# A two-layer image network in fp32: the 3x3 convolution keeps its split planes in a ring, and its element work moves between VectorE, ScalarE and GpSimd

## What is computed

```python
x = x + _L0_conv_ref(_gn(x), ...)     # gate, windowed attention (8x8 windows, 16 heads), projection
x = x + _L1_conv_ref(_gn(x), W, bias) # 3x3 convolution, 128 -> 128 channels, padding 1, plus bias
```

## Time and profile before

| | |
|---|---|
| median of 3 runs | 1300.46 us (1294.46 to 1301.38) |
| profiled execution | 1303.66 us, its span 1301.9 us |
| busy: TensorE matmul | 1058.8 us (81%) |
| busy: VectorE | 1024.6 us (79%) |
| busy: ScalarE | 793.4 us (61%) |
| busy: GpSimd | 605.2 us (46%) |
| mean granted TensorE clock | 0.946 of full speed |

### The profile page before, as it was taken

One profiled execution on the slowest core, in us unless ns is written; L12 is line 12 of the kernel. 1 busy time (PEld: TensorE's weight loads), 2 busy tenths in 40 slices (PEclk: granted clock), 3 DMA queues, 4 the chain that ended last, 5 costly groups with the idle time before them and its releaser, 6 DMA issues. The chain is left out here.

```text
span 1301.9 us, 52825 instructions
## 1 busy us (share of the span) xinstructions
PE 1058.8 (81%) x23011; PEld 582.1 (45%) x23011; DVE 1024.6 (79%) x1315; ACT 793.4 (61%) x1295; POOL 605.2 (46%) x501
## 2 busy tenths in 40 slices
PE   1179999989998975887855999999999998498886
PEld 1045555555555542333322555555555555243332
DVE  6866787778887646999996677777787774599998
ACT  1147877777787764544412777777777776454442
POOL 7004444444444354555541344445445444366665
PEclk9999999999999996999885999999999999698998
DMA  7054444435444400222234544445444441001112
GB/s 284 25 147 122 134 130 132 140 113 145 123 133 127 138 19 1 97 98 97 97 114 139 138 130 137 127 128 140 133 132 129 138 141 30 1 33 48 49 50 80
DMA packets 114918, 140.60 MB, mean 108 GB/s; under 512 B 25088, under 2 KB 91008, under 8 KB 113664
## 3 DMA queue, kind: packets, MB, share of 16 engines
q1 hardware_dynamic: 114688, 137.23, 35.2%
HBM read 67.96 MB, written 67.11 MB: 104 GB/s over the span
## 5 line engine op out<-in xcount | busy, mean ns | idle before, releaser
L646 DVE TENSOR_REDUCE m_all<-ps 128x16 f32<-128x1024 f32 x256 | 312.8, 1222 | 134.2 <-PE ps L855 133.7
L369 POOL TENSOR_TENSOR g_lo<-work,g_hi 128x512 f16<-128x512 f32 x64 | 91.6, 1431 | 301.1 <-ACT g_hi L503 301.1
L361 POOL TENSOR_SCALAR work<-work 128x256 f32<-128x256 f32 x128 | 114.2, 892 | 210.2 <-DVE work L639 191.9
L824 PE MATMUL ps<-work,c_hi 128*128 128x512 f16 x384 | 153.5, 400 | 64.3 <-DVE work L744 64.3
L528 ACT CAST work<-work 128x640 f16<-128x640 f32 x128 | 91.9, 718 | 151.6 <-DVE work L740 118.0
L867 PE MATMUL ps<-q_bd,k_pl 128*64 128x256 f16 x2048 | 164.3, 283 | 18.2 <-DMA q_bd<-m_pair 13.0
L451 ACT ACTIVATE work<-ps,ws 128x1024 f32<-128x1024 f32 x128 | 142.7, 1115 | 40.8 <-PE ps L867 39.0
L855 PEld LDWEIGHTS ps<-k_pl,q_bd 48*64 48x64 f16 x8192 | 88.7, 111 | 155.1 <-issue 75.4
L744 DVE TENSOR_TENSOR work<-work 128x640 f16<-128x640 f32 x128 | 152.3, 1193 | 4.3 <-ACT work L528 4.2
L451 ACT ACTIVATE late_probs<-ps,ws 128x1024 f32<-128x1024 f32 x128 | 141.6, 1106 | 20.4 <-PE ps L867 20.4
L825 PE MATMUL ps<-work,c_lo 128*128 128x512 f16 x384 | 152.7, 398 | 0.0
(11 more groups left out here) (128 smaller groups left out, 2008.7 us busy)
## 6 DMA issues: line engine op xcount, KB each, us to landing
stack_scratch<-work SPq DMA_DIRECT2D x128, 256.0 KB, 2.0
k_pl<-stack_scratch SPq DMA_DIRECT2D x128, 192.0 KB, 3.7
q_bd<-stack_scratch SPq DMA_DIRECT2D x256, 96.0 KB
stack_scratch<-work SPq DMA_DIRECT2D x128, 128.0 KB, 2.1
out_dram<-work SPq DMA_DIRECT2D x32, 512.0 KB, 2.6
img<-in_x_dram SPq DMA_DIRECT2D x8, 1024.0 KB, 13.5
img<-in_x_dram SPq DMA_DIRECT2D x16, 512.0 KB, 4.2
q_bd<-m_pair SPq DMA_DIRECT2D x256, 8.0 KB
```

The lines of the kernel that those rows point to most:

```text
L361: g.tensor_scalar(near[h], near[h], -2.0, None, ALU.add).then_inc(less_done, 1)
L646: v.tensor_reduce(m_all[:, 0, :, p], ps[:, S_B:S_B + 2, :].rearrange("p r (a k) -> p (r a) k", k=WIN), AX.X, ALU.max).then_inc(max_done, 1)
L824: t_.matmul(o, lhs_hi, rhs_hi, start=first, stop=False)
```

## The change

- **Ring.** `x_hi` and `x_lo` become one tile `x_both` of 18 rows per plane. A strip needs 10 rows; even strips use rows 0 to 9, odd strips rows 8 to 17, so two rows serve both. `normed`, the planes, the casts and the remainders therefore handle 8 new rows (the first strip 9) instead of 10. After an odd strip the last two rows are copied to the front by `carry` on VectorE. An even strip's casts still wait for the strip before on TensorE, an odd strip's only for the carry.
- **All four planes** are made on VectorE (`plane_of`), none on GpSimd.
- **Sums.** ScalarE starts both output pixels from bank 1 (`bases`, two instructions; the odd pixel is kept with the opposite sign). VectorE adds banks 0 and 3 in one instruction of 2 x 512 elements (`ends`) and bank 2 to both pixels in another (`middle_sums`).
- **Residual** on GpSimd in two instructions of 512 elements, every second pixel each. Except in the last strips the first half also waits for plane 1 and the second for plane 3 of the strip three further on. The second subtracts, which turns the sign back.
- **Three output buffers**, and the statistics of a refilled strip are taken three strips later instead of two.
- `cx` lies on the first layer's `g_hi`/`g_lo` (`g_both`); `work` grows from 8468 to 9984 fp32 per partition. The zero row of the first strip is now in the fp16 ring.

The core of the diff. The lines that it takes away stand in the kernel above; here only what comes in their place:

```diff
-HALO = CROWS + 2
+XROWS = CROWS + 1
+RING = 2 * CROWS + 2
+OUTS = 3
...
+        g_both = sb("g_both", [P, BUFS * UT])
+        g_hi, g_lo = (g_both[:, :].bitcast(F16)[:, k * BUFS * UT:(k + 1) * BUFS * UT].rearrange("p (s t) -> p s t", s=BUFS)
+                      for k in range(2))
...
+        cx = g_both[:, 0:XROWS * WIDE].rearrange("p (r c) -> p r c", r=XROWS)
+        plane = [part(i * XROWS * (SIDE // 2), XROWS * (SIDE // 2)).rearrange("p (r c) -> p r c", r=XROWS) for i in range(PLANES)]
+        x_both = part(2304, PLANES * RING * (SIDE // 2)).bitcast(F16).rearrange("p (k i r c) -> p k i r c", k=2, i=PLANES, r=RING)
+        x_hi, x_lo = x_both[:, 0, :, :, :], x_both[:, 1, :, :, :]
+        c_out = [part(6912 + i * 1024, 1024).rearrange("p (r c) -> p r c", r=CROWS) for i in range(OUTS)]
...
+        def ring_rows(t):
+            at = CROWS * (t % 2)
+            return slice(at + (1 if t == 0 else 2), at + RING - CROWS)
+        def new_rows(t):
+            return slice(0 if t == 0 else 1, XROWS)
+        def column(t, s):
+            return cx[:, new_rows(t), s:s + SIDE - 1:2]
...
+        def halves(buf):
+            return buf.rearrange("p r (c e) -> p e (r c)", e=2)
...
+                    if more and t == CUNITS - 4:
+                        after(sp, cx_done, (b + 1) * CUNITS - 1)
+                        sp.wait_ge(kept_done, 2)
+                        for e in range(2):
+                            refill(CUNITS - 2 + e, x_in[e])
                     after(sp, cadd_done, n)
                     after(sp, out_done, n - 1)
+                    sp.dma_start(out[b, :, t * CROWS:t * CROWS + CROWS, :], c_out[n % OUTS][:, :, :]).then_inc(out_done, 16)
+                    if more and t < CUNITS - 2:
                         after(sp, cx_done, n + 1)
+                        after(sp, next_in, t - 1)
+                        refill(t, next_in)
...
+                def residual(t, n, spared):
+                    c = outputs_view(n)
+                    x1 = (kept[t - CUNITS + 2] if spared and t >= CUNITS - 2 else img[:, t * CROWS:t * CROWS + CROWS, :])
+                    x1 = x1.rearrange("p r (c e) -> p (r c) e", e=2)
+                    after(pool, sums_out, n)
+                    if t < CUNITS - 4:
+                        after(pool, planes_done, n + 3, 2)
+                    g.tensor_tensor(c[:, :, 0], c[:, :, 0], x1[:, :, 0], ALU.add).then_inc(cadd_done, 1)
+                    if t < CUNITS - 4:
+                        after(pool, planes_done, n + 3, 4)
+                    g.tensor_tensor(c[:, :, 1], x1[:, :, 1], c[:, :, 1], ALU.subtract).then_inc(cadd_done, 1)
...
+                def bases(n):
                     after(act, conv_done, n, 2)
+                    after(act, out_done, n - OUTS)
+                    for e, (col, bias) in enumerate(((R_CONV, vecs[:, 3:4]), (R_MINUS, cf[:, C_MINUS:C_MINUS + 1]))):
+                        a.activation(outputs(c_out[n % OUTS], e), ps[:, PLANES * (n % 2) + 1, :], ACT.Identity,
+                                     scale=ws[:, col:col + 1], bias=bias).then_inc(base_out, 1)
...
+                    def normed(t, n):
+                        after(act, planes_done, n - 1)
+                        last = XROWS - (1 if t == CUNITS - 1 else 0)
+                        r = slice(new_rows(t).start, last)
+                        a.activation(cx[:, r, 1:1 + SIDE], img[:, t * CROWS + r.start:t * CROWS + r.stop, :],
                                      ACT.Identity, scale=cf[:, C_SLOPE:C_SLOPE + 1], bias=cf[:, C_OFF:C_OFF + 1]).then_inc(cx_done, 1)
+                    def high(i, t, n):
+                        after(act, planes_done, n, i + 1)
+                        if t % 2 == 0:
+                            after(act, conv_done, n - 1, i + 1)
+                        elif t > 1:
+                            after(act, carried, carries(b, t - 2))
+                        a.copy(x_hi[:, i, ring_rows(t), :], plane[i][:, new_rows(t), :]).then_inc(x_hi_done, 1)
                     if top:
                         act.wait_ge(coef_ready, 2 * b + 2)
+                        normed(t, n)
+                        for i in range(PLANES):
+                            high(i, t, n)
+                        normed(t + 1, n + 1)
+                    if not top:
+                        bases(n - 1)
                     if not bottom:
+                        for i in range(PLANES):
+                            high(i, t + 1, n + 1)
+                    if t + 2 < CUNITS:
+                        normed(t + 2, n + 2)
+                    if bottom and b + 1 == BATCH:
+                        bases(n)
...
+                v.memset(x_both[:, :, :, 0, :].rearrange("p k i c -> p (k i) c"), 0.0).then_inc(pads_zero, 1)
...
+                def ends(n):
+                    bank = PLANES * (n % 2)
+                    after(dve, base_out, n)
+                    after(dve, conv_done, n)
+                    c = halves(c_out[n % OUTS])
+                    v.scalar_tensor_tensor(out=c, in0=ps[:, bank:bank + PLANES:PLANES - 1, :], scalar=ws[:, R_CONV:R_CONV + 1], in1=c,
+                                           op0=ALU.mult, op1=ALU.add).then_inc(ends_out, 1)
+                def middle_sums(n):
+                    after(dve, ends_out, n)
+                    c = halves(c_out[n % OUTS])
+                    v.scalar_tensor_tensor(out=c, in0=ps[:, PLANES * (n % 2) + 2, :].unsqueeze(1).broadcast_to([P, 2, 512]),
+                                           scalar=ws[:, R_CONV:R_CONV + 1], in1=c, op0=ALU.mult, op1=ALU.add).then_inc(sums_out, 1)
+                def sums(n):
+                    ends(n)
+                    middle_sums(n)
...
+                    def plane_of(i, t, n):
                         after(dve, cx_done, n)
+                        after(dve, x_lo_done, n - 1, i + 1)
+                        if t == CUNITS - 1 and i == 0:
+                            after(dve, planes_done, n - 1)
+                            v.memset(cx[:, XROWS - 1, 1:1 + SIDE], 0.0).then_inc(pads_zero, 1)
                             dve.wait_ge(pads_zero, 4 * b + 4)
+                        l, r, op = ((0, 2, ALU.subtract), (1, 2, ALU.add), (2, 1, ALU.subtract), (1, 3, ALU.subtract))[i]
+                        v.tensor_tensor(plane[i][:, new_rows(t), :], column(t, l), column(t, r), op).then_inc(planes_done, 1)
+                    def low(i, t, n):
                         after(dve, x_hi_done, n, i + 1)
+                        v.tensor_tensor(x_lo[:, i, ring_rows(t), :], plane[i][:, new_rows(t), :], x_hi[:, i, ring_rows(t), :],
+                                        ALU.subtract).then_inc(x_lo_done, 1)
+                    def carry(n):
+                        after(dve, conv_done, n - 1)
+                        after(dve, x_lo_done, n)
+                        flat = x_both.rearrange("p k i r c -> p (k i) (r c)")
+                        w = SIDE // 2
+                        v.tensor_copy(flat[:, :, 0:2 * w], flat[:, :, (RING - 2) * w:RING * w]).then_inc(carried, 1)
                     more = b + 1 < BATCH
                     if top:
+                        for i in range(PLANES):
+                            plane_of(i, t, n)
+                        for i in range(PLANES):
+                            low(i, t, n)
                     if not bottom:
+                        plane_of(0, t + 1, n + 1)
+                        plane_of(1, t + 1, n + 1)
+                    if not top:
+                        ends(n - 1)
+                    if t % 2 and not bottom:
+                        carry(n)
+                    if not bottom:
+                        low(0, t + 1, n + 1)
+                        plane_of(2, t + 1, n + 1)
+                        low(1, t + 1, n + 1)
+                        plane_of(3, t + 1, n + 1)
+                    if not top:
+                        middle_sums(n - 1)
+                    if not bottom:
+                        low(2, t + 1, n + 1)
+                        low(3, t + 1, n + 1)
+                    if more and t > 2:
+                        strip_stats(t - 3)
                     if more and bottom:
+                        for k in range(CUNITS - 3, CUNITS):
+                            strip_stats(k)
                     if bottom and not more:
+                        sums(n)
...
+                        if i == 0 and t and t % 2 == 0:
+                            after(pe, carried, carries(b, t - 1))
+                        after(pe, (ends_out, base_out, sums_out, ends_out)[i], n - 2)
                         for k in range(ROW_TAPS):
                             q = i * ROW_TAPS + k
+                            rows = slice(CROWS * (t % 2) + k, CROWS * (t % 2) + k + CROWS)
+                            mm = three(ps[:, bank, :], c_hi[:, q, :], c_lo[:, q, :], x_hi[:, i, rows, :], x_lo[:, i, rows, :],
                                        first=(k == 0), last=(k == ROW_TAPS - 1))
```

177 lines of the change are left out of this document (30 added, 147 removed).

## The result

| | before | changed |
|---|---|---|
| median (lowest to highest, 4 runs each) | 1300.92 us (1294.46 to 1309.67) | 1249.74 us (1246.44 to 1260.63) |
| profiled execution, span | 1303.66, 1301.9 us | 1246.97, 1245.3 us |
| mean granted TensorE clock | 0.946 | 0.962 |

The ratio is 0.9617, with an interval of 0.9533 to 0.9701: faster by 3 to 4.7%. The forecast was 1242, the range 1233 to 1260.

The account below looks back on a forecast made before the run. VectorE was taken to bound both batches, partly standing still behind GpSimd. Per strip batch 0 falls from 10.69 to 8.75 us, batch 1 to TensorE's 7.78; gains 22.4 and 36.2, together 58.6, give 1242 us, range 1233 to 1260.

Parts of the forecast that it names:

- terms 1, 2, 5 and 6: Per strip: VectorE's planes and low parts 4.80 us, sums 2.40, batch 0's statistics 1.20; ScalarE's 5.4 hidden beside 7.8.
- Term 4: GpSimd's two residual halves, 1.17 us each, run under VectorE's 1.2 us sums, leaving 0.10 us of wait per strip.
- rival A: GpSimd's halves outlast their cover: at 1.8 us each, VectorE waits 0.55 twice a strip; 1263 us, chance 0.12.
- Batch 1 becomes TensorE's: Second layer, batch 1: VectorE needs 7.55 us per strip, so TensorE's 7.78 sets the pace.
- Term 3: VectorE's copy of 1024 fp16 elements in every second strip: taken as 0.5 us, or 0.25 per strip.
- Batch 0 in steps: Second layer, batch 0: step 4 begins at 541.3 us, eleven steps of 8.75 follow, end 8.2; gain 22.4.
- Batch 1 in steps: Second layer, batch 1: TensorE begins strip 2 at 1148.64, fourteen strips of 7.78 end at 1257.6; gain 36.2 us.
- fall into the slack: Last strips of batch 1: the residuals without gates were to cost nothing.
- the idleness leaves: TensorE in batch 1: its idle stretch goes, so no clock fall, costing 1.7 us, is counted.
- B: TensorE's clock keeps falling, four times in batch 1: +7 us, 1249, chance 0.14.
- C: The hand-over between ScalarE, VectorE and TensorE binds, 0.9 us lost per pair of strips: +6 in batch 1, 1248, chance 0.08.
- D: Slower: GpSimd halves above about 2.6 us eat the gain; at 3.0 us each +14, so 1314 us, chance 0.04.

Follow-up runs that it names:

- tiny residual: Changed kernel with the two GpSimd residual halves working on 16 of 512 elements each, the rest left out, all waits kept: 1236.90 us.
- second timing: The changed kernel unaltered, timed once more: 1255.44 us, ratio 0.9659.
- coupled casts: Changed kernel with the odd strips' casts also made to wait for TensorE, plane by plane: 1262.93 us.

## Why the prediction was right or wrong

**What bounds the kernel, and the sign: right.** VectorE bound both batches by its own work and by standing still behind GpSimd. Taking elements off it and putting GpSimd under the sums made the kernel faster by 3.8%, and 1249.74 us lies within the range, 7.7 above the forecast. Planes 0.68, sums 1.27, casts 0.62, normalization 1.25: terms 1, 2, 5 and 6 came within 0.05 us.

**Term 4 failed: the halves.** It took 1.17 us from half of L387, whose inputs and output are contiguous, and said so only in rival A ("nothing in the trace writes every second fp32 on GpSimd"). The row that I used against A, L399, reads one shared stretch; the residual reads two. And even contiguous halves take 1.28, since half of a long instruction is not a short one: 16 elements still take 0.23. (The 1.43 of term 4's mean comes from one row of 2.86; the mean of L387 is 2.90, so 1.45.) At 1.51 they outlast the 1.2 us sums, and 0.10 us of wait per strip became 0.75. Rival A was the mechanism, its size was milder: waits of 0.40 and 0.35 us instead of 0.55 twice. It took the wait as the half less 1.25 us; the rows have 0.40 and 0.35 at 1.51, so the half less 1.11 to 1.16.

**"Batch 1 becomes TensorE's" failed with it.** VectorE needs 8.56 - 1.20 + 0.75 = 8.11 us there, measured 8.13 (7.96 and 8.31), more than TensorE's 7.78. TensorE set the pace only for strips 2 to 8, until VectorE's lead was gone. With halves of 1.28 it did become TensorE's, as the contiguous and the tiny residual show. The tolerance stood in the prediction's own numbers: 7.55 and 7.78 leave 0.23 us, less than what the two ends of term 4 left open.

**Term 3, the carry:** 0.33 us in its row (0.17 per strip) instead of 0.5; alone it is busy 0.42, in the kernel with the tiny residual and in the one with two buffers. Those are the two ends of what the prediction estimated by the Trainium skill ("VectorE: DVE Perf Modes", the section on the perf-mode tier table), four elements a cycle; the trace agrees, and my interpolation from fp32 rows was the worse guide. The 0.8 of the row above is 0.42 and a wait for GpSimd.

**Batch 0 in steps.** The loop's step 4 began 47.4 us after the aggregation, 0.2 before the forecast. The nine steps up to step 13 took 83.6 us instead of 78.8: 4.9 lost. Term 4 alone lost 0.65 a step, 5.9; the cheaper carry and its neighbours gave about 1 back. The last two steps with the ungated residuals took 19.5 instead of 21.9: only one of them met remainders, for 1.7 us (626.71), so 2.4 was won. The end took 10.2 instead of 8.2, since the refill was awaited 2.8 us and not 1.0. Together 4.1 us less gain than predicted, 18.3 instead of 22.4.

**Batch 1 in steps.** TensorE was through with its last matmul 142.2 us after the aggregation instead of 137.5. It began strip 2 1.2 us earlier than assumed. Then five strips of 8.17 us lost 2.0, and strip 14 took 10.2 us, 2.4 lost by the ungated halves, which did not "fall into the slack", because there was none. The fall of the clock in strip 15 cost 1.7, which the prediction had put at nothing on the ground that the idleness leaves; one stretch of it stayed. In the second timing no fall followed that stretch, but 14 matmuls instead of 7 ran at the lower clock at the start, and the sum was the same. The end took 9.0 instead of 8.1, two halves of 1.49 in place of 2.5 among it. Together 5.6 less, 30.6 instead of 36.2.

**The total was better than its terms.** The forecast of the profiled execution, 1245.1, came within 2 us of 1246.97 only because the first layer was 7.8 us short in it. That is luck. The median before less the 48.8 us of the second layer, 1252, is what the mechanism gives. The two medians, 1249.74 and 1255.44, lie around it, and the second has a kernel before of 1303.88 beside it, which less 48.8 is 1255.1.

**The other rivals.** B: from strip 2 to strip 14 of batch 1 no matmul was at the lower clock (1.00 in the window), although the banks are cycled as before; one fall came, behind the longest idle stretch of that batch's run of strips, and in the second timing of the same kernel the same stretch (2.15 us) brought none. C: the hand-over never bound. With the residual taken out, the only wait left on VectorE in mid-batch 1 is 0.46 us for the normalization, once in two strips, with TensorE busy throughout, and the coupled casts changed nothing. D would have wanted halves of 2.6 us; ungated ones do reach 3.70, and even that kernel stayed 2% below the kernel before.

## What to carry to other kernels

Work that is hidden under an instruction of another engine has to be measured in the very form in which it will run; its margin is the cover less its price, and half of a longer instruction with another layout was 0.34 us off a margin of 0.03. Moving work off an engine that disturbs a neighbour paid here, as far as the runs show, mostly through the freedom to place what remains. The gates without the third buffer gave back 34 of 49 us, and the third buffer without the gates 21. Where a stage that was not touched differs by several microseconds between two executions, compare stages, and not totals.

## What the runs showed of the hardware

- GpSimd's fp32 sum of 512 elements takes 1.04, 1.28 or 1.51 us by the layout of its inputs, and the step of its output changes nothing.
- A VectorE instruction with two SBUF inputs and a GpSimd half do not run side by side: the remainder behind a sum took 1.08 us instead of 0.68 where the half had begun first, and where two-input instructions had begun first they kept their pace (1.28 us for two) and the half took 3.70 us instead of 1.51.
- While GpSimd works, a VectorE copy of fp16 in SBUF waits as a two-input instruction does: L765 0.81 instead of 0.42. A sum with one input in PSUM keeps its 1.27.
- TensorE's granted clock fell behind idle stretches of 2.03 us and 2.15 us, but not behind every one: in batch 0 2.31 us brought no fall, nor did the 2.15 us in the second timing. In 100 us without a gap (contiguous halves, batch 1) it did not fall.
- The first layer, with the same instructions, took 438.8 to 453.3 us over all kernels here, and 440.2 and 445.5 in two executions of one kernel; the second layer of those two differed by 0.3 at most.
